# Last attention of four: scores as nine exact bf16 products stacked along the contraction, the terms spread through DRAM, and the shift copied into the query rows by ScalarE

## The reference

```python
def _L3_xattn_ref(x, mask, kv, kv_mask, Wq, bq, Wk, bk, Wv, bv):
    q = jnp.einsum('oc,bct->bot', Wq, x) + bq[None, :, None]
    k = jnp.einsum('oc,bct->bot', Wk, kv) + bk[None, :, None]
    v = jnp.einsum('oc,bct->bot', Wv, kv) + bv[None, :, None]
    ...
    attn = jnp.einsum('bhqd,bhdk->bhqk', q * scale, k)
    attn = jnp.where(kv_mask[:, :, None, :], attn, -jnp.inf)
    attn = jax.nn.softmax(attn, axis=-1)
    mean = jnp.einsum('bhqk,bhkd->bhqd', attn, v)
    ex2 = jnp.einsum('bhqk,bhkd->bhqd', attn, v * v)
    std = jnp.sqrt(jax.nn.relu(ex2 - mean * mean))
    ...
    return (xn * std + mean) * mask
```

## Time and profile before

| | |
|---|---|
| median of 3 runs | 1072.5 us (1072.28 to 1078.0) |
| span of the profiled execution | 1069.8 us |
| around the span | about 2.7 us, if the profiled execution took the median |
| busy: PE, PEld, DVE, ACT, POOL | 90%, 56%, 51%, 44%, 26% |
| mean granted clock of PE | 0.975 |
| DMA | 60.14 MB, 56 GB/s |

### The profile page before, as it was taken

How to read it: one execution, slowest core, us unless ns; L and a number is a source line. 1 busy time by engine, 2 the same in 40 slices (tenths; PEclk the granted TensorE clock), 3 DMA queues, 4 the chain that set the end, 5 groups by cost and what they waited for, 6 DMA issues and landing times.

```text
span 1069.8 us, 21418 instructions
## 1 busy us (share of the span) xinstructions
PE 965.6 (90%) x8560; PEld 600.5 (56%) x8560; DVE 545.0 (51%) x1036; ACT 471.2 (44%) x808; POOL 275.1 (26%) x389
## 2 busy tenths in 40 slices
PE   7989999999999999999999999999999999985673
PEld 5566663666456664666636664556646666344430
DVE  3343565455645565445644556455654556543433
ACT  2424453453534545345534545345543455333223
POOL 0230230342211621233302422116212333023201
PEclk9999999999999999999999999999999999988867
DMA  9300230001300202102300113002121022002001
GB/s 369 147 2 1 80 104 23 18 22 64 109 30 6 80 28 87 36 2 84 109 19 19 40 46 109 31 5 80 40 76 36 2 85 99 18 19 79 6 1 40
DMA packets 29057, 60.14 MB, mean 56 GB/s; under 512 B 9376, under 2 KB 21024, under 8 KB 24096
## 3 DMA queue, kind: packets, MB, share of 16 engines
q1 hardware_dynamic: 28960, 58.77, 15.1%
HBM read 53.52 MB, written 5.24 MB: 55 GB/s over the span
## 4 chain that ended last, share of the span: by engine, by line
PE 74%; DVE 11%; issue 7%; ACT 4%; POOL 2%; DMA 1%; SPq 0%; DVEq 0%; ACTq 0%; POOLq 0%
PE GP L598 6%; PE GP L999 6%; PE PV L737 6%; PE GP L1010 6%; PE GP L600 5%; PE SC L805 5%; DVE nm L1455 4%; PE SC L720 4%; PE GP L983 3%; PE PV L776 3%; PE PV L930 3%; PE GP L822 2%; PE GP L605 2%; PE SC L917 2%; PE MX L653 2%
## 5 line engine op out<-in xcount | busy, mean ns | idle before, releaser
L1455 DVE TENSOR_REDUCE nm<-MX 128x2 bf16<-128x512 f32 (+1 forms) x352 | 227.1, 690 | 147.2 <-PE MX L659 59.0
L1229 ACT ACTIVATE Pr<-SC,bcol 128x1024 f32<-128x1024 f32 x64 | 71.2, 1113 | 137.0 <-PE SC L805 126.1
L1786 POOL TENSOR_TENSOR Psum<-Pr 128x512 f32<-128x512 f32 x64 | 81.4, 1272 | 173.6 <-ACT Pr L1229 173.6
L598 PE MATMUL GP<-zP,W 128*128 128x128 f32 x512 | 106.9, 291 | 7.1 <-DMA W<-w 7.1
L1229 ACT ACTIVATE Pr<-SC 128x1024 f32<-128x1024 f32 x64 | 65.3, 1020 | 81.9 <-PE SC L720 42.4
L600 PE MATMUL GP<-uP,W 128*128 128x128 f32 x512 | 100.3, 278 | 0.0
L598 PEld LDWEIGHTS GP<-zP,W 128*128 128x128 f32 x512 | 78.8, 194 | 28.5 <-issue 26.7
L1270 ACT ACTIVATE Pr<-SC,bcol 128x512 f32<-128x512 f32 x96 | 60.7, 684 | 58.6 <-PE SC L917 58.6
L1754 POOL TENSOR_TENSOR stat<-stat,half 128x1 f32<-128x1 f32 x24 | 13.7, 569 | 267.7 <-DVE stat L1635 172.5
L600 PEld LDWEIGHTS GP<-uP,W 128*128 128x128 f32 x512 | 79.2, 195 | 0.0
L1010 PE MATMUL GP<-WB,work 128*128 128x256 f32 x256 | 62.5, 394 | 10.5 <-DVE work L1583 10.5
(11 more groups left out here) (202 smaller groups left out, 1733.8 us busy)
## 6 DMA issues: line engine op xcount, KB each, us to landing
WA<-w1a SPq DMA_DIRECT2D x8, 1024.0 KB, 4.8
WB<-w1b SPq DMA_DIRECT2D x8, 1024.0 KB, 7.2
WA<-w2a SPq DMA_DIRECT2D x8, 1024.0 KB, 5.0
WB<-w2b SPq DMA_DIRECT2D x8, 1024.0 KB, 7.1
W<-w SPq DMA_DIRECT2D x6, 1024.0 KB, 10.0
scratch<-U SPq DMA_DIRECT2D x16, 256.0 KB, 2.0
C<-scratch SPq DMA_DIRECT2D x96, 32.0 KB
zP<-z_in SPq DMA_DIRECT2D x8, 128.0 KB, 4.4
```

Source lines behind the costliest of these rows:

```text
L598: pe.matmul(dst, W0[:, piece, 2 * s, at:at + P], zP[:, s * P:s * P + P], start=True, stop=False)
L1229: act.activation(Pr[:, n % 4:n % 4 + 2, :], SCP[:], ACT.Exp, bias=bcol[:, 3 + k % 2:4 + k % 2] if L else 0.0, scale=8.0 ** -0.5 if L else ...
L1455: dve.tensor_reduce(dst, MX[(n + i) % 2][:].rearrange("p (a k) -> p a k", a=a), AX_X, ALU.max, negate=True).then_inc(mx_done, 1)
L1786: pool.tensor_tensor(Psum[:, c % 4, :].rearrange("p (a l) -> p a l", l=D), two[:, :, 0:D], two[:, :, D:2 * D], ALU.add)\
```

## The change

- A query or key is split into three bf16 terms, high, rest and rest of the rest (`parts`). For queries DVE makes them from the bank of `q3` (four operations in a row, `queries3`); for keys ACT makes the high term, DVE the rest, GpSimd the other two.
- SP stores `parts` to DRAM and loads it back so that 72 partitions of `Qx` and `Kx` hold, for each head, all nine pairs of terms: partition 24 j + 8 i + d of `Kx` has term j of dimension d, the same of `Qx` term i. Partition 72 of `Kx` takes the key mask, against a row of ones in `Qx`. Partitions 96 to 99 of `Qx` take the negated maxima, against rows of an identity in `Kx`, which GpSimd writes once at the start, after two memsets.
- A score is then one bf16 matmul over 100 rows and 256 columns, and a maximum is one over 96 rows of the same tiles.
- The turned maxima of L3 are copied by ACT (`shift3`), 4 partitions of 256, repeated for 4 heads, from MX into `Qx`; DVE's copy is gone, and so is the Exp's bias.
- `BOTH` has another order, with a step `(None, 0, ...)` without scores.
- `W0` has five slots. The weights of the values share slot 4 and are loaded twice a batch by SP (`load_values`): those of vp2 and vp3 after x1, behind `WA` and `WB`, those of vp0 and vp1 after the inputs.
- The second MLP buffer is gone (`G = T`), the loads of `w1a`, `w1b` and the inputs now stand behind the two `terms` on SP's queue, and the two loads and one operation for the mask column are gone.

```diff
@@ BOTH, the order of the mixed stretch
         (0, 4, [(0, 3, 2)], [("den", 1), (0, 3, "T"), ("recip", 0, 0), ("recip", 0, 1)]),
-        (0, 5, [(3, 0, 0)], []), (0, 6, [(3, 0, 2)], []), (0, 7, [("den", 2), (3, 0, "T")], [(3, 1, 0)]),
+        (0, 5, [], [(0, 0, "B")]), (0, 6, [], [(0, 1, "B")]),
+        (0, 7, [(3, 0, 0)], [(3, 0, 2), ("den", 2)]),
+        (None, 0, [], [(3, 0, "T"), (3, 1, 0)]),
         (3, 0, [], [(3, 1, 2)]),
-        (3, 1, [("den", 3), (3, 1, "T"), ("recip", 1, 0)], [(0, 0, "B")]),
-        (3, 2, [(0, 1, "B"), ("recip", 1, 1)], [("out", 0), (3, 2, 0)]),
-        (3, 3, [("out", 1), (3, 2, 2)], [("out", 2), ("out", 3), (3, 2, "T")]),
-        (3, 4, [(0, 2, "B")], [(3, 3, 0)]),
-        (3, 5, [(3, 3, 2), ("out", 4)], [("out", 5), (3, 3, "T")]),
-        (3, 6, [(0, 3, "B")], []), (3, 7, [("out", 6), ("out", 7)], [])]
+        (3, 1, [("den", 3), ("recip", 1, 0), ("recip", 1, 1)], [(3, 1, "T"), (3, 2, 0)]),
+        (3, 2, [("out", 0), ("out", 1)], [(3, 2, 2), ("out", 2)]),
+        (3, 3, [(3, 2, "T"), ("out", 3)], [(0, 2, "B"), (3, 3, 0)]),
+        (3, 4, [], [(3, 3, 2), (0, 3, "B")]),
+        (3, 5, [("out", 4)], [("out", 5), (3, 3, "T")]),
+        (3, 6, [("out", 6)], [("out", 7)]), (3, 7, [], [])]
@@ SP
+            def load_values(n):
+                sp.wait_ge(s_V0, 2 * n)
+                sp.dma_start(W0[:, 4], w0[4 + n % 2]).then_inc(ld_w0v, 16)
+            def terms(b, dst, scr, ready, stored, landed, key_side):
+                sp.wait_ge(ready, b + 1)
+                sp.dma_start(scr.rearrange("i d (h l) -> (d h) i l", l=D), parts[:]).then_inc(stored, 16)
+                if key_side:
+                    sp.wait_ge(s_msk, N_MSK * b + 3)
+                    sp.dma_start(dst[72:73], b3row[0:1, :].unsqueeze(1).to_broadcast([1, NH, D])).then_inc(landed, 16)
+                sp.wait_ge(stored, 16 * b + 16)
+                for j in range(3):
+                    src = scr[j:j + 1].to_broadcast([3, 8, NH * D]) if key_side else scr
+                    sp.dma_start(dst[24 * j:24 * j + 24], src).then_inc(landed, 16)
             def body(b):
                 sp.wait_ge(s_x1, b + 1)
                 load_mlp(w2a, w2b)
+                if not is_last(b):
+                    load_values(2 * b + 3)
                 if not is_first(b):
                     store_batch(b - 1)
+                terms(b, Kx, k_parts, s_K3l, st_k, ld_kx, True)
+                terms(b, Qx, q_parts, s_Q3l, st_q, ld_qx, False)
                 if not is_last(b):
-                    sp.wait_ge(s_x3, b + 1)
                     load_mlp(w1a, w1b)
                     load_inputs(b + 1)
                     if b + 2 < B:
                         load_z(b + 2)
+                        load_values(2 * b + 4)
@@ PE
-                    pe.wait_ge(ld_w0[4 + w], 16)
+                    pe.wait_ge(ld_w0v, 16 * (2 * k + w + 1))
@@ maxima_pair3
+                        h = HG * g + u + i
+                        for s in range(2):
+                            mm = pe.matmul(MX[(n + i) % 2][:, s * D:s * D + D], Qx[0:96, h, s * P:s * P + P],
+                                           Kx[0:96, h, :], start=True, stop=True, skip_group_check=True)
@@ scores3
+                    for e in range(2):
+                        h = HG * g + 2 * j + e
+                        mm = pe.matmul(SC[j][:, e * D:e * D + D], Kx[0:100, h, kc * P:kc * P + P], Qx[0:100, h, :],
+                                       start=True, stop=True, skip_group_check=True)
@@ ACT
+            def shift3(b, units):
+                for _, g, _ in (unit for unit in units if unit[0] == 3 and unit[2] == "T"):
+                    n = MX_AT[b, 3, g, "T"]
+                    act.wait_ge(mx_full[n % 2], n // 2 + 1)
+                    act.activation(Qx[96:100, HG * g:HG * g + HG, :], MX[n % 2][:].bitcast(BF16)[96:100, 0:D]
+                                   .unsqueeze(1).to_broadcast([HG, HG, D]), ACT.Copy).then_inc(nmQ_ready, 1)
@@ DVE
+            def queries3(b, o):
+                g = take(o, "q3")
+                dve.wait_ge(st_k, 16 * b + 16)
+                dve.tensor_scalar(parts[:, 0, :], g[:, 0:D], col("bq"), None, ALU.add).then_inc(s_Q3h, 1)
+                rest(g, "bq", rest_q, (s_Q3h, b + 1)).then_inc(s_Q3r, 1)
+                dve.wait_ge(s_Q3r, b + 1)
+                dve.tensor_copy(parts[:, 1, :], rest_q).then_inc(s_Q3m, 1)
+                dve.wait_ge(s_Q3m, b + 1)
+                dve.tensor_tensor(parts[:, 2, :], rest_q, parts[:, 1, :], ALU.subtract).then_inc(s_Q3l, 1)
@@ DVE, in attention 2, before quotient(b, 2, 0)
+                rest(take(o, "k3"), "bk", rest_k, (s_K3h, b + 1)).then_inc(s_K3r, 1)
@@ GpSimd, before power(b, 3)
+            def keys3(b):
+                pool.wait_ge(s_K3r, b + 1)
+                pool.tensor_copy(parts[:, 1, :], rest_k).then_inc(s_K3m, 1)
+                pool.wait_ge(s_K3m, b + 1)
+                pool.tensor_tensor(parts[:, 2, :], rest_k, parts[:, 1, :], ALU.subtract).then_inc(s_K3l, 1)
@@ GpSimd, at the start
+            pool.memset(Qx[64:96], 1.0).then_inc(const_x, 1)
+            pool.memset(Kx[64:96], 0.0).then_inc(const_x, 1)
...
             pool.wait_ge(const_p, 3)
+            pool.wait_ge(ld_par, 48)
+            for g in range(NG):
+                pool.tensor_copy(Kx[96:100, HG * g:HG * g + HG, :],
+                                 ident[96:100, 96:100].unsqueeze(2).to_broadcast([HG, HG, D])).then_inc(const_x, 1)
+                pool.wait_ge(const_x, 3 + g)
             additions0(0, range(8))
```

More of the change, by code:

```diff
@@ L110, in mix @@
             units(b, end)
-            sc.extend((b + (L == 0), L, 2 * k + i) for i in range(2))
+            if L is not None:
+                sc.extend((b + (L == 0), L, 2 * k + i) for i in range(2))
     def banks0(b, names):
@@ L144 @@
 SC_AT = {unit: n for n, unit in enumerate(SC_SEQ)}
-SHIFTS = [unit[:3] for unit in MX_SEQ if unit[3] == "T"]
+SHIFTS = [unit[:3] for unit in MX_SEQ if unit[3] == "T" and unit[1] != 3]
 def reduced(n):
     return sum(isinstance(unit[3], int) for unit in MX_SEQ[:n + 1])
-N_MSK = 7
+N_MSK = 6
 V_STEPS = 4 + 4
@@ L226, in build @@
         Q12 = work[:, 0:8 * P].rearrange("p (h l) -> p h l", l=P)
-        Q3 = work[:, 8 * D:12 * D].rearrange("p (t l) -> p t l", l=D)
-        X, T, G = (work[:, 1024 * i:1024 * i + 1024] for i in range(3))
+        X, T = (work[:, 1024 * i:1024 * i + 1024] for i in range(2))
+        G = T
         zP = sb("zP", [P, D])
@@ L250, in build @@
         nm3 = sb("nm3", [P, 2, 2, P], BF16)
-        nmT3 = sb("nmT3", [P, 2, D], BF16)
         U3 = sb("U3", [P, NG, D])
-        lat, junk, rec = (U3[:, i, :] for i in range(1, 4))
+        rest_q, lat, junk, rec = (U3[:, i, :] for i in range(4))
+        rest_k = junk
         x0 = zR[:]
@@ L504, in _ @@
             sp.dma_start(uP[:], ctx_in[0]).then_inc(ld_proj, 16)
-            for i in (0, 2, 4, 1, 3, 5):
-                sp.dma_start(W0[:, i], w0[i]).then_inc(ld_w0[i], 16)
+            for i in (0, 2, 4, 1, 3):
+                sp.dma_start(W0[:, i], w0[i]).then_inc(ld_w0[i] if i < 4 else ld_w0v, 16)
                 if i == 0:
@@ L851, in mixed @@
                             denominators(b + 1, k // 2 - 1)
-                    else:
+                    elif L == 3:
                         scores3(b, k)
@@ L859, in mixed @@
                             pv0(b + 1, at)
-                        else:
+                        elif before == 3:
                             pv3(b, at)
@@ L1134, in body @@
                 pe.matmul(g[:, 0:D], W3[:, 0, :], x3[:], start=True, stop=True).then_inc(full, 1)
-                mixed(b, range(4, 16) if more else range(8), make03)
+                mixed(b, range(4, len(BOTH)) if more else range(8), make03)
                 mix_end(b)
@@ L1373, in keys3 @@
                     g = take(o, "k3")
-                    for e in range(2):
-                        ins = act.activation(K3[:, e, :], g[:, 0:D], ACT.Identity, scale=hmask[:, 8 + e:9 + e],
-                                             bias=col("bkm", e))
-                    ins.then_inc(s_K3, 1)
+                    wait(act, st_q, 16 * b)
+                    act.activation(parts[:, 0, :], g[:, 0:D], ACT.Identity, bias=col("bk")).then_inc(s_K3h, 1)
                 attention12(b, 2, 0.25, keys3)
@@ L1393, in body @@
                     cast(b + 1, 3)
-                mixed(b, range(4, 16) if more else range(8))
+                mixed(b, range(4, len(BOTH)) if more else range(8))
                 mix_end(b)
@@ L1594, in layer_norm, with rest @@
                     .then_inc(s_xb, 1)
+            def rest(g, bias, dst, high):
+                dve.wait_ge(*high)
+                return dve.scalar_tensor_tensor(out=dst, in0=g[:, 0:D], scalar=col(bias), in1=parts[:, 0, :],
+                                                op0=ALU.add, op1=ALU.subtract)
+            def queries3(b, o):
[7 more added lines that the diff above has]
```

(9 more changed lines are left out.)

169 lines of the change are left out of this document (63 added, 106 removed), and 4 rows, old and new, of the table TAKEN.

## The result

The changed kernel takes 1141.6 us (median of 4 runs, 1140.4 to 1145.5) against 1072.5 before: ratio 1.064, 95% interval 1.061 to 1.067, so 6% slower; the prediction was 1134. Its profiled execution has a span of 1139.9 us, 70.1 more than before.

A forecast was written before the change was run, and what follows sets the result against it. PE's queue order was taken to bound batches 0 to 6. Mixed stretch 18.2, value weights 36.4, subtraction 3.2 and last batch 3.5 sum to 61 us, giving 1134 us, range 1097 to 1160.

The forecast's parts named there:

- value weights, wait: Before vp2 in batches 0 to 6: PE waits 3.7 us for the value load queued behind WB.
- value weights, slow clock behind: Matmuls after the vp2 wait run partly at 1.2 GHz: 1.5 us a batch added (bounds 0 and 2.5).
- subtraction ahead of the quotient: Key path: DVE's new subtraction sits before the quotient the chain waits on, 0.4 x 8 = 3.2 us.
- mixed stretch: PE's rewritten stretch, 399.04 to 439.96 us before: waits 12.2 against 3.8, matmuls save 5.8, so +2.6 us a batch.
- last batch: Nothing covers the query path there, +6 us; cheaper scores give back 2.5 at the end: +3.5.
- start: GpSimd's two memsets and four copies before its first addition: taken as costing nothing.
- rival of a load in time: Value load overtakes or runs beside WB, so vp2 doesn't wait: 1098 us, chance 0.08.
- Hidden, by 2.9 us: Query path, x3 to first maxima: loads land at about 407.0, PE reaches (3,0,0) at 409.9.
- rival with three engines: Three engines appear only for the key path, hidden even so (7.5 us); queries late had chance 0.22.
- rival of a held start: GpSimd's four start copies run at 2.1 ns an element and delay the first addition: +14, 1148 us, chance 0.12.
- PE stays the bound: Mixed stretch loses its 5.8 us a batch, copies and reductions hidden behind pv and out work: 1063 us, chance 0.10.

The follow-up runs named there:

- early load: Changed kernel with the load of the second value weights (vp2, vp3) issued before the wait for x1, ahead of WA and WB: 1103.1 us, 1.030.
- quarter-copy run: Changed kernel with ACT's copy of the transposed shift cut to one head of four (256 elements a partition instead of 1024): 1119.1 us, 1.044.
- new order: Changed kernel with only the units of the mixed stretch reordered, other work put behind most T's: 1105.4 us, 1.033.
- early load and new order: Changed kernel with second value load before x1's wait, mixed stretch reordered, and first value reload ahead of the masks at the start: 1059.7 us, 0.988.
- old order: Changed kernel with `BOTH`, the order of units, taken from the kernel before: 1169.4 us, 1.089.
- best order with a quarter of the copy: Kernel with early load and new order, with ACT's shift copy cut to one head of four: 1053.6 us, 0.981.

## Why the prediction was right

The sign, the places and the mechanism held, and the sum was 9 us short of the span's growth (7.6 of the medians'). Term by term, over the execution (us):

| term | predicted | measured |
|---|---|---|
| value weights, wait | 3.7 x 7 = 26 | 28.9, of 3.76 to 5.00 |
| value weights, slow clock behind | 1.5 x 7 = 10.5 | 13.3 |
| subtraction ahead of the quotient | 3.2 | 2.8 |
| mixed stretch | 2.6 x 7 = 18.2 | 18.3 |
| last batch | 3.5 | 5.7 |
| start | 0 | 1.1 |
| sum | 61 | 70.1 |

The seven first halves gained 45.0. The early load takes away 42.2 of it, of which 28.9 are the waits and 13.3 the clock; the 2.8 that stay, 0.4 a batch, are the subtraction's. The kernel before with five slots shows the first two rows without the new attention: its first halves gained 42.6, with 30.2 of waits.

**Value weights.** Right as to cause and sizes, and the rival of a load in time is out: in the batch shown it lands 9.4 us after WB's issue, for the 9.5 that I laid out. The clock was undersized by 0.4 a batch, and only in part of them. In batches 1, 3 and 4 the window of 5.45 us behind the wait has a granted clock of 0.51 to 0.54, over vp2's matmuls and attention 2's first maxima, and the half lost 2.3 to 2.5 us to it. In the other four the same window has 0.69 to 0.72, and they lost 1.4 to 1.6, as I had it from the earlier trace rows. What decides between the two wasn't found.

**The mixed stretch.** The net, 2.6, met 2.25 in the quiet batches (41.30 - 39.05), but out of parts that were off and canceled, and the 18.3 of all batches is the sum of +4.1 and +4.9 in batches 0 and 2, 2.0 to 2.5 in four others and 0.4 in batch 6. So the agreement with 18.2 is luck. The parts:
- Matmuls: I had -5.8. At full clock, in the quarter-copy run, PE is busy 32.05 where it was 37.30: -5.2. Scores have steps of 0.44 to 0.54, as said; a pair of maxima takes up to 0.54 instead of 0.44, which I had put at no change.
- Waits: I had 12.2 against 3.8, so +8.4. The windows have 7.7 against 1.75, so +5.9. Behind the T's of groups 0 and 1 I had 1.33; it is 0.89, because half a pair of maxima runs on the other bank while ACT copies. Between two pairs I had 0.74 twice, and there is next to none: both (3,0,2) and (3,3,2) start with their first half (574.34 and 592.32 above). This is the step that failed in size: my schedule let a pair wait for both banks before its first matmul, as in the kernel before, and in the new `maxima_pair3` each half waits for its own bank alone. ACT's copy itself was right (1.02 for 1.0), the wait of the quotient's spreading nearly (1.51 for 1.75).
- Clock: I counted none in this stretch. It costs 1.6 by the quarter-copy run (33.63 against 32.05), 1.2 by the new order's 32.44; batches 0 and 2, with granted clocks of 0.92 and 0.88, are 1.8 and 2.5 longer still.

The second half of batch 6 adds only 0.4 instead of 2.6: attention 1 of the last batch lies in it, 28.8 us at a granted clock of 0.87 before and 27.2 at 0.93 after, which gives 1.6 back.

**The query path.** "Hidden, by 2.9 us" was nearly wrong. I had 5.7 us from store to landing; it is 7.5 to 8.5. Of it the 2.06 to the loads' issue was right, the landing wasn't: 4.2 to 5.3 us from the third load's issue at its end instead of 2.4. By the 7.70 us of the early load and new order (an estimate, since PE doesn't wait there) they land at 572.2 in the timeline above, 0.6 before PE asks for them at 572.78; by the 8.48 of the old order they would have been late. In the last batch nothing covers the path: the step from q3 to the first maxima grew from 1.76 to 9.98, +8.2 where I had 6. What follows is 2.3 shorter (2.5 predicted). The rival with three engines is out: 12 small packets a load. The Trainium skill's rule (DMA: Bandwidth & Descriptors, Why a DMA increments its semaphore by 16 and not by 1) gives 12 for 24 merged rows, and this trace agrees, as far as small packets tell the engines.

**The start.** The rival of a held start is out, and for a simpler reason than I argued: a copy has 1024 elements a partition, not 4096, and takes 1.08 us, 1.06 ns an element. The 1.1 us that I put at nothing are PE's wait for the first reload of the value weights, behind the masks, which I hadn't followed.

**The other side.** "PE stays the bound" needed waits under 4 us in the mixed stretch and a value load in time. Both were to be had, in another order: with waits of about 3 us and the load early the kernel takes 1059.7. That this is close to the 1063 that I gave this rival is chance, since its sum had the load still late and would be 1037 with the load early. The mixed stretch gained 3.4 us a batch (39.05 to 35.6), not the 5.8 of the saved matmuls: those came to 4.9 (37.30 to 32.45), and the waits are still 1.4 longer than the old 1.75. The last batch is 12.3 us longer than before in that trace. What spoke against the rival, T's with nothing behind them, was a property of the order, not of the operations.

## What to carry to other kernels

When a change saves work on the engine that bounds, write down for each saved piece what it used to cover; here 5.2 us of matmuls a batch went, and 5.9 us of waits and 1.6 us of slow clock came in their place, until the order was laid anew. Try a load that has become periodic in the queue at the moment when its buffer comes free, and not behind the loads whose trigger happens to be near: here the same bytes cost 44 us in one place and none in another. And look at what the change frees as well as at what it moves: a slot of SBUF was paid for on a DMA queue.

## What the runs showed of the hardware

Short waits can cost more than their length. In the mixed stretch of the changed kernel, 7.7 us of waits in 41.3, none longer than 1.51, went with a granted clock of 0.96 and 1.2 to 1.6 us of longer matmuls; with 5.5 us in 37.6 (a quarter of the copy) and with 3.4 in 35.8 (the new order) it stayed at 1.00. The sum of the waits doesn't settle it alone: in batch 0 of the quarter-copy run, with 5.8, the clock is 0.96, and in batch 2 of the best order with a quarter of the copy it is below full with fewer waits than any of these, none longer than 0.90:

```profile
391.23:427.57 36.34, 33.56 (x288) 17.08 (x287) 20.62 (x33) 15.35 (x20) 5.11 (x5) 0.95 0.43 141
```

The last batch, sparse in every kernel, changes its length with the clock. From its first MLP to the last transfer the changed kernel takes 105.4 us, and 112.0 in the early-load run, where the code there is the same: the granted clocks of the first MLP's half, the second MLP and the stretch to the end are 0.81, 0.81, 0.66 in the one and 0.75, 0.64, 0.58 in the other. These are not two fixed lengths. To the end of the span, with the same code in the last batch, it is 107.1 in the changed kernel and 107.2 with the old order, 113.7 and 113.8 in the two runs with the early load and 115.4 with the new order alone. Whether that comes of the batches ahead, which have fewer waits in the last three, or differs from one execution to the next isn't shown, for each run has one trace. The four executions of the early-load run take 1100.9 to 1108.8, and the best kernel's six 1054.9 to 1065.9, which the last batch may explain.
